# Self-attention of sixteen 8-wide heads on one core: steps of a pair of heads with separate PSUM bank pairs for plain and turned scores, softmax sums from a ones column in the value stationaries

## Time and profile before

| | us |
|---|---|
| median of 3 runs | 1531.94 (1529.16 to 1536.08) |
| span of the profiled execution | 1525.2 |
| its own time | not listed apart from the runs |
| first attention, from its first score to the next phase | 27.8 to 480.5 |
| the rest after it | 1044.7 |

### The profile page before, as it was taken

One profiled execution on the slowest core, in us unless ns is written; L12 is line 12 of the kernel. 1 busy time (PEld: TensorE's weight loads), 2 busy tenths in 40 slices (PEclk: granted clock), 3 DMA queues, 4 the chain that ended last, 5 costly groups with the idle time before them and its releaser, 6 DMA issues. The chain is left out here.

```text
span 1525.2 us, 56397 instructions
## 1 busy us (share of the span) xinstructions
PE 1317.3 (86%) x22833; PEld 839.9 (55%) x22834; DVE 930.2 (61%) x2397; ACT 706.0 (46%) x1485; POOL 770.9 (51%) x1355
## 2 busy tenths in 40 slices
PE   3899999999987978999999999697899996892786
PEld 2455555555555653555555555465555553662676
DVE  3566676666665554766677676455477766674333
ACT  1354655555454434655566656243344442430443
POOL 3233233333322573877787787578322222586455
PEclk9999999999999998999999999799899999996899
DMA  3350000000000135334352434022111101321221
GB/s 78 67 149 14 25 14 18 21 18 17 11 27 9 56 103 159 100 101 120 84 135 70 135 101 106 19 76 71 35 29 36 35 23 42 107 91 70 71 80 47
DMA packets 145313, 97.92 MB, mean 64 GB/s; under 512 B 20533, under 2 KB 141964, under 8 KB 145068
## 3 DMA queue, kind: packets, MB, share of 16 engines
q1 hardware_dynamic: 142252, 88.06, 21.1%
q0 software_dynamic: 2816, 6.37, 1.1%
HBM read 40.31 MB, written 54.61 MB: 62 GB/s over the span
## 5 line engine op out<-in xcount | busy, mean ns | idle before, releaser
L622 ACT ACTIVATE space<-scores 128x512 f32<-128x512 f32 x576 | 314.2, 552 | 336.9 <-PE scores L481 222.0
L708 DVE TENSOR_REDUCE space<-scores 128x2 f32<-128x512 f32 (+1 forms) x512 | 306.7, 622 | 216.9 <-PE scores L481 149.0
L857 POOL TENSOR_SCALAR_AFFINE_SELECT space<-space 128x512 f32<-128x512 f32 x128 | 81.5, 637 | 271.7 <-ACT space L622 271.7
L452 PE MATMUL scores<-space 32*128 32x256 f32 (+1 forms) x2304 | 195.2, 407 | 22.2 <-DVE space L708 15.7
L481 PE MATMUL scores<-space 32*128 32x256 f32 (+1 forms) x2048 | 151.4, 358 | 1.2 <-issue 1.2
L869 POOL TENSOR_TENSOR space<-space 128x1024 f32<-128x1024 f32 x64 | 151.4, 2366 | 0.0
L452 PEld LDWEIGHTS scores<-space 32*128 32x128 f32 x2304 | 96.0, 190 | 88.9 <-DVE space L708 77.3
L861 POOL TENSOR_SCALAR_AFFINE_SELECT space<-space 128x512 f32<-128x512 f32 x128 | 87.4, 683 | 73.1 <-ACT space L622 73.1
L481 PEld LDWEIGHTS scores<-space 32*128 32x128 f32 x2048 | 84.9, 187 | 19.0 <-issue 2.1
L166 DVE BATCH_NORM_STATS2 space<-space 128x6 f32<-128x128 f32 (+1 forms) x304 | 66.8, 272 | 22.1 <-DMA space<-xo 17.2
L477 PE MATMUL scores<-space,selectors 32*128 32x256 bf16 (+1 forms) x1024 | 73.3, 256 | 6.5 <-issue 5.0
(11 more groups left out here) (324 smaller groups left out, 2908.1 us busy)
## 6 DMA issues: line engine op xcount, KB each, us to landing
by_expert<-blank SPq DMA_DIRECT2D x33, 1040.0 KB, 9.4
space<-by_expert SPq DMA_DIRECT2D x40, 130.0 KB
space<-in_x SPq DMA_DIRECT2D x32, 128.0 KB, 2.3
space<-xx SPq DMA_DIRECT2D x32, 128.0 KB, 2.4
xo<-space SPq DMA_DIRECT2D x32, 128.0 KB, 2.3
space<-xo SPq DMA_DIRECT2D x16, 256.0 KB
space<-xm SPq DMA_DIRECT2D x32, 128.0 KB, 2.3
w_w<-in_L_ffn_w SPq DMA_DIRECT2D x8, 256.0 KB
```

The source lines that it names most:

```text
L452: last = pe.matmul(a.score_bank(j)[:, 0:n], q[rows, e * P:(e + 1) * P], keys[rows, 0:n], start=not cut, stop=True, skip_group_check=True)
L622: act.activation(pt[:, 2 * pair:2 * pair + 2, lo:S], a.score_banks(pair)[:, :, S + lo:2 * S], ACT.Exp, bias=0.0, scale=1.0)\
L708: last = dve.tensor_reduce(out[:, c % 2, 2 * pair:2 * pair + 2], banks[:, :, 0:n], AX.X, ALU.max, negate=True)
L857: pool.affine_select(out=block, in_=block, compare_op=ALU.is_ge, fill=0.0, base=0, pattern=[[0, 4], [1, P]], channel_multiplier=-1).then_i ...
```

## The change

The first attention gets a class and engine functions of its own (FirstAttention, tensor_first_attention and so on). `SelfAttention` keeps its work for the second layer and loses the branches for G = 1. `split` becomes a function, `split_maxima`, with the same five operations. What the new functions do otherwise:

- A step is now (b, c, p): quad c of batch b, and of it one pair of heads p, that is two strips, with both blocks of queries. There are again ten steps to a batch. The turned scores in slot i are those of step i - 9, so they are always of the other pair of strips.
- The bank pair scores[0] holds plain scores only (128 + 256 columns for each strip, 512 in a cross step), the pair scores[1] turned scores only (256 + 128, or 512). In a slot TensorE issues the triangles of the plain scores, the selectors of the turned ones, and then, for each e, the plain scores of the pair and the turned ones of the other pair.
- VectorE's maxima and ScalarE's exponential of a slot don't wait for each other. There is one exponential for a step.
- Cross steps use selectors and keys of 128 columns in place of twice 64.
- The value stationaries have a 1 in column 16 or 17 beside the values, so the numerator's matmul sums the exponentials too. The matmuls of L522 and L505 are gone. ScalarE writes the values into zeroed stationaries with plain copies; GpSimd zeroes them and sets the ones once.
- Own results are summed in `num`, cross results in `turned[0]`. VectorE transposes both first, then takes reciprocals, multiplies, and transposes back.
- In the phase that routes tokens to experts, a few unused columns of `rows` are set to zero once.

```diff
+    CROSS, PER, LAG, LATER = QUADS, 10, 9, 2
+    PIECES = {1: [(N, 1, -1, 1), (T, 0, 1, 0)], 3: [(V, 0, 0, 1)], 5: [(N, 0, 0, 0), (Q, 0, 1, 1)], 7: [(K, 0, 1, 0)], 9: [(Y, 0, -2, 1)]}
+    STEPS = {8: [(S, -1)], 0: [(X, -2)], 1: [(U, -2)], 2: [(M, -2)], 3: [(R, -2)]}
+    KEYS = {7: (0, 1), 8: (2, 4), 9: (3, 5), 0: (6, 7)}
...
+    def triangles(p):
+        for part in range(4):
+            for j in (2 * p, 2 * p + 1):
+                out = a.score_bank(j)[:, 0:4 * P].rearrange("p (e t) -> p e t", t=S)[:, :, 32 * part:P]
+                pe.matmul(out, k.ident_parts[rows(j), part], k.above_parts[rows(j), part, 32 * part:P].unsqueeze(1).to_broadcast([32, 2, P - 32 * part]),
+                          start=(part == 0), stop=False, skip_group_check=True)
...
+    def shifts(t):
+        b, c, p = a.unit(t)
+        lows = a.maxima(a.part(t))
+        for e in range(2):
+            for j in (2 * p, 2 * p + 1):
...
+                    pe.matmul(a.turned_bank(j)[:, e * S:S + e * P], k.selectors[rows(j), c % 2], lows[rows(j), e * P:S],
+                              start=(e == 0), stop=False, skip_group_check=True)
...
+    def window(i):
+        t = i - a.LAG
+        wait(pe, s["maxed"], min(i, a.PER * B))
+        wait(pe, s["exped"], t)
+        if a.is_window(i):
...
+            if c < a.CROSS:
+                triangles(p)
+        if a.is_window(t):
+            wait(pe, s["max_ready"], a.part(t) + 1)
+            shifts(t)
+        for e in range(2):
+            if a.is_window(i):
+                last = scores(i, e)
+            if a.is_window(t):
+                last = turned_scores(t, 1 - e)
+        last.then_inc(s["window"].sem, 1)
...
+            for e in range(2):
+                for j in range(4):
+                    own = 128 * j + 64 * (c // 2) + at
+                    last = pe.matmul(strip(k.num, j)[:, half + e * P:half + S], k.own_val[:, b % 2, e, own:own + 32], pt[:, j, e * S:S + e * P],
+                                     start=(c == 0 and e == 0), stop=(c % 2 == 1 and e == 1), skip_group_check=True)
...
+    def exps(i, t):
+        b, c, p = a.unit(t)
+        unit, n = (QUADS + 1) * b + c, a.turned_width(c)
+        wait(act, s["window"], i + 1)
+        wait(act, s["pv_done"], unit - 1)
+        act.activation(k.pairs[:, unit % 2, 2 * p:2 * p + 2, 0:n], k.scores[1][:, :].rearrange("p (j t) -> p j t", j=2)[:, :, 0:n], ACT.Exp,
+                       bias=0.0, scale=1.0).then_inc(s["exped"].sem, 1)
...
+        if kind == a.V:
+            wait(act, s["v_full"], b + 1)
...
+            act.copy(k.own_val[:, b % 2].rearrange("p e (n x) -> p (e n) x", x=32)[:, :, 0:8], bank[:, 0:S].rearrange("p (n x) -> p n x", x=8))
+            for half in range(2):
+                part = slice(64 * half, 64 * half + 64)
+                last = act.copy(k.vx[part, b % 2].rearrange("p e (j x) -> p e j x", x=32)[:, :, :, 8 * half:8 * half + 8],
+                                bank[part, S:S + P].rearrange("p (j e h x) -> p h e j x", j=4, e=2, h=2)[:, half])
...
+            dve.tensor_reduce(out[:, :, 0, c % 2], banks[:, :, 0:P], AX.X, ALU.max, negate=True)
+            last = dve.tensor_reduce(out[:, :, 1, c % 2], banks[:, :, P:P + S], AX.X, ALU.max, negate=True)
...
+        if kind == a.S:
+            wait(dve, s["pv_done"], (QUADS + 1) * b + QUADS)
+            wait(dve, s["scaled"], b)
+            dve.transpose(turned(0), blocks(k.num[:, :])).then_inc(s["own_turned"].sem, 1)
+        if kind == a.X:
...
+            dve.transpose(turned(1), blocks(k.turned[0][:, :])).then_inc(s["cross_turned"].sem, 1)
...
+            dve.reciprocal(k.rsums, groups[:, :, 16:18]).then_inc(s["rden"].sem, 1)
...
+            dve.transpose(k.out_turned[:, :].rearrange("p g t -> p (g t)"), k.out_heads).then_inc(s["ot"].sem, 1)
...
-            for j in range(4):
-                pe.matmul(strip(k.turned[0], j)[:, lo:S], k.ones_column[:, c], pt[:, j, lo:S], start=first, stop=done,
-                          skip_group_check=True)
-            for j in range(4):
-                last = pe.matmul(strip(k.num, j)[:, lo:S], of(j), pt[:, j, lo:S], start=first, stop=done, skip_group_check=True)
...
-        if kind == a.V and a.G == 1:
-            wait(dve, s["v_full"], b + 1)
-            wait(dve, s["pv_done"], a.per * (b - 1))
-            own_values(bank, b, 0)
...
-CONSTANTS = 38
+CONSTANTS = 30
```

More of the change, by code:

```diff
@@ L459, in turned_scores @@
         wait(pe, s["max_ready"], a.part(t) + 1)
-        q, keys = a.queries(b, c), a.keys(b, c)
-        if c == a.CROSS:
-            for half in range(2):
-                for j in range(4):
-                    rows, out = slice(32 * j, 32 * j + 32), slice(64 * half, 64 * half + 64)
-                    pe.matmul(a.score_bank(j)[out, S:2 * S], k.selectors[rows, 2 + 2 * e + half, 0:TC], a.maxima(t)[rows, :],
-                              start=True, stop=False, skip_group_check=True)
-            for half in range(2):
-                for j in range(4):
-                    rows, out, at = slice(32 * j, 32 * j + 32), slice(64 * half, 64 * half + 64), (2 * e + half) * TC
-                    last = pe.matmul(a.score_bank(j)[out, S:2 * S], keys[rows, at:at + TC], q[rows, :],
-                                     start=False, stop=True, skip_group_check=True)
-            return last
-        lo = e * P if a.mask == "before" else 0
         blk = a.keys_block(e)
@@ L502, in values @@
         strip = lambda x, j: x[32 * j:32 * j + 32]
-        if c == a.CROSS:
+        blk = a.keys_block(e)
+        of = lambda j: k.val[:, b % 2, blk, 32 * (4 * c + j):32 * (4 * c + j) + 32]
+        half = c % 2 * S
+        if e == 0:
+            wait(pe, s["num_saved"], QUADS * b + c)
             for j in range(4):
-                pe.matmul(strip(k.turned[0], j)[:, S:2 * S], k.ones_cross[:, e], pt[:, j, :], start=False, stop=(e == 1),
+                pe.matmul(strip(k.num, j)[:, half:half + P], of(j), pt[:, j, 0:P], start=True, stop=False,
@@ new lines, in values @@
+        wait(pe, s["masked"], a.masks(n))
+        to = half + (1 - e) * P
+        for j in range(4):
+            last = pe.matmul(strip(k.num, j)[:, to:to + P], of(j), pm[:, j, :], start=False, stop=(e == 1),
+                             skip_group_check=True)
+        if e == 1:
+            if c == 0:
+                wait(pe, s["den_saved"], b)
+            wait(pe, s["summed"], QUADS * b + c + 1)
+            for j in range(4):
+                last = pe.matmul(strip(k.turned[0], j)[:, b % 2 * S:(b % 2 + 1) * S], k.ones_column[:, c], k.both[:, c % 2, j],
+                                 start=(c == 0), stop=(c == 3), skip_group_check=True)
@@ L558, in piece @@
                 last = pe.transpose(bank[:, blk * P:(blk + 1) * P], k.wn[:, b % 2, blk], k.ident[:, :])
-            if a.ctx is not None:
-                wait(pe, s["ctx_in"], 16 * (b + 1))
-                last = pe.transpose(bank[0:CC, S:S + TC], k.ctx_in[:, b % 2], k.ident[0:TC, 0:TC])
             last.then_inc(s["t_full"].sem, 1)
@@ L610, in exps @@
     def exps(i, t):
-        b, c, e = a.unit(t)
-        lo = e * P if a.mask == "before" and c < a.CROSS else 0
         pt = k.pt[:, t % TURNED]
@@ L616, in exps @@
         wait(act, s["pv_done"], t - TURNED + 1)
-        if a.mask == "after":
-            wait(act, s["summed"], (t - TURNED) // 2 + 1)
+        wait(act, s["summed"], (t - TURNED) // 2 + 1)
         for pair in (1, 0):
@@ L679, in scalar_self @@
             piece(kind, n, b, which)
-        for kind, n, b, which in a.pieces(i - 1):
-            if kind == a.K:
-                own_keys(a.bank(which), b, (2, 3))
-        for kind, n, b, which in a.pieces(i - 2):
-            if kind == a.K:
-                cross_keys(a.bank(which), b)
 def vector_self(dve, a):
@@ L728, in save_denominators @@
         wait(dve, s["rden"], b)
[L729 to L732 removed]
+        dve.transpose(k.den[:, 0:S], k.turned[0][:, b % 2 * S:(b % 2 + 1) * S]).then_inc(s["den_saved"].sem, 1)
     def step(kind, n, b):
[L736 removed]
         if kind == a.U:
@@ L801, in vector_self @@
             step(kind, m, b)
-        for kind, m, b, which in a.pieces(i - 1):
-            if kind == a.V and a.G == 1:
-                own_values(a.bank(which), b, 1)
-                cross_values(a.bank(which), b).then_inc(s["v_ready"].sem, 1)
         ahead = i // a.per + 2
@@ L873, in gpsimd_self @@
             if a.part_end(part) == i:
-                split(part)
-        if a.is_unit(i - a.lag) and a.unit(i - a.lag)[1] < a.CROSS:
+                split_maxima(pool, a, part, 2, 2 * a.part_end(part))
+        if a.is_unit(i - a.lag):
             mask(i - a.lag)
-            if a.mask == "after" and (i - a.lag) % 2 == 1:
+            if (i - a.lag) % 2 == 1:
                 add(i - a.lag)
```

618 lines of the change are left out of this document (386 added, 232 removed).

## The result

The changed kernel takes **1515.62 us** as the median of four runs (1507.41 to 1526.24), the kernel before 1532.04 on the same chip (1529.16 to 1536.08): a ratio of 0.9899, with an interval of 0.9852 to 0.9946. The forecast was 1519, in a range of 1498 to 1548. Measured once more with five rounds it was 1513.44, ratio 0.9854 (0.9804 to 0.9903). The number was good, but by luck: of the steps behind it one was too dear, one left out the largest loss, and the two nearly cancelled.

What follows compares the result with a forecast made beforehand. The first attention was taken as bound by its scores-maxima-scores ring, not engine totals. Opening 21.6 + middle 391.2 + end 18.6 = 431.4 us against 444.4, 13.0 less than the median 1531.9: 1519, range 1498 to 1548.

Steps and rivals of the forecast that it cites:

- ring: Each step of the first attention goes scores, maxima, scores; a wide step before: 1.39 + 0.08 + 1.37 + 0.05 = 2.89 us.
- TensorE's part: Triangles, shifts and two score phases of a step: 1.29 us with the first shift after the triangles, 1.18 beside them.
- the maxima: VectorE's two maxima per step of a pair, 0.42 and 0.69 us with a little overlap: 1.08 us; 1.23 in cross steps.
- Costed at nothing: Changes to value matmuls, VectorE's remaining work, ScalarE and GpSimd counted as hidden, except 0.1 us in a batch's second step.
- the twins: Ones-column value matmuls L522 and L505: removing them saves 3.8 us of TensorE a batch, covered by the maxima, worth nothing.
- VectorE's other work: Value spreading, transposes and reciprocals stand behind the maxima in each step; no cost except 0.1 us in a batch's second step.
- own step: A step of the changed first attention with triangles: 1.29 + 0.08 + 1.08 + 0.05 = 2.50 us.
- independent strips: Rival: each strip runs on alone, the first shift hides beside the triangles, 13.5 us more gain: 1505, chance 0.17.
- The head: Nine opening steps of plain scores alone, 8 x 2.39 + 2.44 = 21.6 us, against 18.5 before.
- The tail: Nine closing steps of turned scores alone, seven near 2.0 us and two near 2.4: 18.6 us, against 17.0 before.
- No change: Rival: small waits in the first attention take back the gain, 0.8 us a batch: 1530, chance 0.20.
- Two strips at a time: Rival: plain and turned scores do not run beside each other; step 3.36 us, kernel 1654; slower 0.18, full serialization 0.08.

Runs made afterwards that it cites:

- the run without them: Kernel before with all but one of the ones-column matmuls of each kind removed, denominators wrong: 1525.84 us, ratio 0.9991.
- the run with two and two: Changed kernel with both plain score phases of a slot issued ahead of both turned ones: 1516.77 us, ratio 0.989.
- its help: Changed kernel with extra unused whole-array matmuls: 17 before the phase, two in each of two slots, three in each of the first nine steps: 1493.7 us, ratio 0.9784.
- the same strips: Changed kernel with a lag of ten steps instead of nine, so plain and turned scores of a slot use the same pair of strips: 1913.63 us.
- help in head and tail: Changed kernel with extra whole-array matmuls before the phase, in the first nine steps, and in seventeen slots at the stage's end: 1489.67 us, ratio 0.9771.
- two-strip ones: Changed kernel with extra matmuls before the phase, those in the first nine slots on the slot's own two strips only: 1508.28 us, ratio 0.9865.
- same strips and four whole-array matmuls a step: Changed kernel with lag ten, extra matmuls at the start, and four whole-array matmuls ahead of each later step: one run, 1792.75 us.

## Why the prediction was right, and where it was not

**What bounds.** Right in the main: the step is a ring of TensorE's part and the maxima, and engine totals decide little: 2.5 us of TensorE taken from a batch of the kernel before moved it by 0.28. But "a shorter TensorE part of a step or shorter maxima, and nothing else" is wrong for the kernel before. Its gaps were not all short: 3.01 us a batch, and 1.64 of the 2.57 gained came out of them. The sum did not suffer by it, since it builds the new step from its own terms.

**Costed at nothing.** Right for the twins, by the run without them. The exponential ends 0.21 inside the maxima, near to what was said (0.95 under 1.08). VectorE's other work stays behind the maxima: the 0.1 allowed in the second step was not needed, that step takes 2.35 like its neighbours.

**The maxima.** 1.02 against 1.08. Alone they take 0.42 and 0.68 (0.42 and 0.69); they overlap by 0.08 (203.09 + 0.42 against 203.43). That is 0.06 of the 0.15 by which the own step was too dear.

**TensorE's part.** This is the step that was mis-sized: "1.29 with the first shift after them. I take 1.29". Measured 1.19, 0.10 less, in every own step. The forecast's other value, 1.18, was near the true one, and the rival built on it, independent strips, is the mechanism. The argument against it, "no row shows two kinds of matmul beside each other", was true of rows that could not have shown it, as there all four strips always had the same kind.
The Trainium skill, page "TensorE: Matmul & The Clock Gate", section "Part 3: Packing small matmuls — row/col tiling", has matmuls start and end strictly in program order. The starts in the traces disagree for matmuls on different strips: 201.97 before 202.26 in the run with two and two, and 202.03 (L548) before 202.10 (L534) in the changed kernel, where the plain one is issued first.

**The steps.** Own 2.35 (2.50), eighth 2.52 (2.70), cross 2.58 and 2.51 (2.66), from first matmul to first matmul. 7 x 2.35 + 2.52 + 2.58 + 2.51 = 24.06, measured 24.05, forecast 25.62. Over 151 steps, 2.562 - 2.405 = 0.157 each makes 23.7 us more gain than forecast.

**The head.** The other failed step: "8 x 2.39 + 2.44 = 21.6", from rows at an assumed clock of 1.00, and with it the last sentence, "78% busy in the head still had 1.00". The column was empty of information there, and the durations in the same trace had told it: 582 ns and 634 ns for matmuls that take 375 to 400 later. From the first score to the first turned score the head took 59.93 - 28.30 = 31.6; with its help 50.30 - 27.42 = 22.9, most of its steps the 2.3 to 2.4 forecast, so the working of the step was nearly right and the clock was what was missing. The help moved the end of the stage by 15.7 us.

**The tail.** Forecast 18.6, measured 427.01 to 450.56, 23.5. Its own steps at the upper level take the 2.0 forecast; the clock falls at 438, which the sum had not reckoned with.

**Together.** Head 31.6 in place of 21.6, middle (59.93 to 427.01) 367.1 in place of 391.2, tail 23.5 in place of 18.6, and a start 0.5 later: -13.0 + 10.0 - 24.1 + 4.9 + 0.5 = -21.7, where the traces have -21.6. The middle holds 3.9 more than 151 x 2.405, by the slow steps up to 76, much as the 4.3 of disturbances that the sum had kept. That 1519 came so near is the luck of these opposite errors. The two ends, 16.0 us by the table, hide two fifths of what the middle gained.

**The rivals.** "No change" named small waits that take back the gain in the batch; the batch shows none that do. "Strips fully independent" had the mechanism, but with 1505 not the time: it, too, left the head at the upper level. "Two strips at a time" was priced fairly: TensorE's part 2.15 against 1.98, a step 3.36 against 3.11. Its point, that the issue order could bring it about, is wrong: even plain ones all ahead of turned ones run side by side. It takes the same strips to get there. What it lacked is the clock, which made that case 1914 (1818 to 1943) instead of the 1654 it gave.

**The whole.** The stage gained 21 us, the medians 16 to 19. The difference is within what the rest of the kernel varies by, 9 to 21 us between two profiled executions and that of before. That the rest is slower because of the change is not shown, and the trace with help in head and tail speaks against it: 1051.6.

## What to carry to other kernels

Before a stretch enters a sum, compare the mean duration of one and the same matmul in it and in the steady part: it tells the clock where the column does not. When work is regrouped so that a lead-in runs on half of the array, price that lead-in at the lower clock as well, and try whether a few matmuls on the whole array, in time in which TensorE waits, hold the upper level. In a ring of two engines, count what lies on the ring, the gaps between the two included, and look at which third engine stands just inside it: here 0.21 us.

## What the runs showed of the hardware that was not expected

- Matmuls on different row strips of TensorE pass each other: one issued later starts 0.29 us earlier, and different kinds (selector, triangle, scores; bf16 and fp32) start 30 to 70 ns apart. Issuing them two and two costs 0.36 us a batch.
- TensorE can be busy 444 of 455 us and stay at 1.2 GHz, with two of four strips at work. Whole-array matmuls put into the head kept the upper level there, two-strip ones only in part (low from 31.7 to 48.8 against until 76 with none). That it matters how much of the array works fits the heads; it was not isolated, and one stretch does not fit by itself: with same strips and four whole-array matmuls a step the clock stayed low from 53 to 97 before it rose.
- The recorded clock of a profile reads 1.00 until its first recorded change, even where matmuls of 375 ns take 629.
- The rest of the program, which no experiment touches, took 1051.6 to 1073.9 us in the thirteen profiled executions, nearly in the order of its mean granted clock, 0.94 to 0.91.
